# An adapter layer on one core: rows of 512 bytes for x and W, half of the first batch's x turned on VectorE, two reorderings at the third chunk and at the end

## What is computed

```
x = x + (x @ B0[id].T) @ A0[id].T                    # id: one of 64 adapters per batch, rank 16
logits = x @ Wr.T + 5 * one_hot(language)             # 8 experts
gates  = softmax over the two largest logits
x = x + x @ W.T + 2 * sum_e gates[e] * (x @ A[e].T) @ Bm[e].T    # rank 16, W is 2048 x 2048
```

## Time and profile before

| | us |
|---|---|
| median of 3 runs | 1563.22 (1560.31 to 1563.93) |
| the profiled execution | 1561.31 |
| its span | 1559.5 |

### The profile page before, as it was taken

The page is one execution under the profiler, slowest core; times in us unless marked ns, Lnnn a source line. Parts: engine busy times, 40 slices in busy tenths (PEclk is TensorE's granted clock), DMA queues, the critical chain, the costliest instruction groups (busy, mean ns, idle before and its releaser), DMA issues.

```text
span 1559.5 us, 20275 instructions
## 1 busy us (share of the span) xinstructions
PE 1541.5 (99%) x7430; PEld 1298.3 (83%) x7430; DVE 1230.4 (79%) x1692; ACT 714.2 (46%) x911; POOL 79.7 (5%) x119
## 2 busy tenths in 40 slices
PE   9989999999999999999999999999999999999998
PEld 8778878888888888888888888888888888888887
DVE  6998878977799767887688776997769976787665
ACT  6522222544445444455445444454444554445442
POOL 2333331000000000000000000000000000000000
PEclk9999999999999999999999999999999999999999
DMA  9899999787777767687676977667776777666564
GB/s 263 224 276 281 265 254 246 215 230 205 218 231 220 216 196 231 219 229 220 203 224 196 257 207 218 216 205 231 209 218 226 215 217 195 214 219 217 198 219 160
DMA packets 303109, 347.04 MB, mean 223 GB/s; under 512 B 204890, under 2 KB 236682, under 8 KB 302346
## 3 DMA queue, kind: packets, MB, share of 16 engines
q1 hardware_dynamic: 293602, 314.28, 69.8%
q0 software_dynamic: 9136, 30.94, 6.0%
q10 hardware_dynamic: 272, 0.52, 0.1%
HBM read 278.52 MB, written 66.72 MB: 221 GB/s over the span
## 4 chain that ended last, share of the span: by engine, by line
PE 88%; DVE 5%; SPq 4%; DMA 2%; issue 1%; ACT 0%; DVEq 0%; ACTq 0%
PE pb L804 26%; PE pb L805 26%; PE pb L806 26%; PE pb L378 4%; PE pb L380 3%; PE pb L533 2%; SPq L669 2%; SPq L292 2%; DVE raw L684 1%; DVE xl L558 1%; DMA out_dram<-ost 1%; DVE pool_a L540 1%; DMA raw<-in_L_cond_W_dram 0%; DMA an<-in_L_cond_A_dram 0%; PE pb L319 0%
## 5 line engine op out<-in xcount | busy, mean ns | idle before, releaser
L796 ACT CAST wh<-raw 128x1024 fp32r<-128x1024 f32 (+1 forms) x453 | 475.4, 1049 | 705.3 <-PE pb L806 670.9
L800 DVE TENSOR_TENSOR wl<-raw,wh 128x1024 fp32r<-128x1024 f32 (+1 forms) x453 | 552.1, 1219 | 261.3 <-ACT wh L796 260.0
L804 PE MATMUL pb<-wh,sh 128*128 128x512 f32 x1568 | 612.8, 391 | 0.5 <-DVE ost L858 0.5
L805 PE MATMUL pb<-wl,sh 128*128 128x512 f32 x1568 | 611.6, 390 | 0.0
L806 PE MATMUL pb<-wh,sl 128*128 128x512 f32 x1568 | 611.2, 390 | 0.0
L806 PEld LDWEIGHTS pb<-wh,sl 128*128 128x128 f32 x1568 | 294.3, 188 | 62.8
L804 PEld LDWEIGHTS pb<-wh,sh 128*128 128x128 f32 x1568 | 294.5, 188 | 56.2 <-DVE wl L800 0.9
L805 PEld LDWEIGHTS pb<-wl,sh 128*128 128x128 f32 x1568 | 294.6, 188 | 55.1
L378 PE MATMUL pb<-awb,xah 128*128 128x304 f32 x512 | 139.0, 305 | 0.3 <-DVE xal L355 0.3
L380 PE MATMUL pb<-awb,xal 128*128 128x256 f32 x512 | 134.6, 280 | 0.0
L804 PE MATMUL pb<-wh,xh 128*128 128x512 f32 x256 | 101.5, 396 | 0.8 <-DVE xl L558 0.8
(11 more groups left out here) (153 smaller groups left out, 1258.6 us busy)
## 6 DMA issues: line engine op xcount, KB each, us to landing
raw<-t_scr SPq DMA_DIRECT2D x392, 512.0 KB, 4.1
xst<-in_x_dram SPq DMA_DIRECT2D x448, 64.0 KB, 3.8
out_dram<-ost SPq DMA_DIRECT2D x72, 256.0 KB, 3.5
raw<-in_L_cond_W_dram SPq DMA_DIRECT2D x124, 128.0 KB, 5.3
raw<-bt_scr SPq DMA_DIRECT2D x28, 512.0 KB, 3.6
out_dram<-u SPq DMA_DIRECT2D x56, 256.0 KB, 2.9
t_scr<-raw POOLq DMA_DIRECT2D x32, 256.0 KB, 4.4
t_scr<-tst POOLq DMA_DIRECT2D x16, 512.0 KB, 6.7
```

The lines of the kernel that those rows point to most:

```text
L796: e.copy(pair_split(wh, g), pair_source(g)).then_inc(c_wh, 1)
L800: e.tensor_tensor(out=pair_split(wl, g), in0=pair_source(g), in1=pair_split(wh, g).bitcast(f32), op=ALU.subtract).then_inc(c_wl, 1)
L804: e.matmul(o, h, wh[:, g % RING, k, :], start=start, stop=False)
L805: e.matmul(o, h, wl[:, g % RING, k, :], start=False, stop=False)
```

## The change

1. x (batches 1 to 7), half of batch 0's x, W and B0's columns are loaded in rows of 512 bytes (128 numbers), where rows of 64 numbers were used. A row then holds two pairs of feature tiles: the transposes take every fourth number of a row (`r` and `h` in the patterns) where they took every second. The tile order of A, Wr, B0 and A0 follows.
2. In batch 0, blocks 1, 3, 5 and 7 of x are loaded in the stream layout by four DMAs each and turned by VectorE (`x_turn_first`); TensorE and ScalarE turn and copy only blocks 0, 2, 4 and 6.
3. W comes in 32 units of 512 KB. Two units make two slots, so `w_turn` of an even tile needs both. Units have three places in turn: `raw` 0 and 1 and `xst` 1 (units 2 and 3 lie in `xst2`). Turns of odd tiles, and two `x_turn` at once in odd slots, stand at the head of their slot. x of batch 1 then has one place in `xst`.
4. In slot 28 the evacuation of the third chunk's last two tiles stands before `pair_lo` in VectorE's list.
5. The last slot's matmuls are ordered by token tile, and the last sum and its stores are done tile by tile.

```diff
-        x_b = x.rearrange("b (h v j) (c k a n) -> b h c k a j v n", h=2, j=32, c=4, k=2, a=4)
-
-        def x_block(m):
-            return xst[:, m % 2, :, :].rearrange("p t n -> p (t n)")
+        x_b = x.rearrange("b (h v j) (c a n) -> b h c a j v n", h=2, j=32, c=4, a=4)
+
+
+        def x_block(n, m):
+            return xst[:, m % 2 if n > 1 else 0, :, :].rearrange("p t n -> p (t n)")
+
+        def wait_x(e, n, m):
+            if n == 1:
+                e.wait_ge(d_x[0], 64 * (m + 1))
+            else:
+                e.wait_ge(d_x[m % 2], (0 if m % 2 else 512) + 64 * (4 * (n - 2) + m // 2 + 1))
...
-            e.transpose(two(n, q, kp).rearrange("p (g j) -> p g j", g=16),
-                        x_block(m).rearrange("p (g i h) -> p h g i", g=16, h=2)[:, u % 2, :, :]).then_inc(c_xc, 1)
+            e.transpose(two(n, q, kp).rearrange("p (r v j) -> p r v j", r=2, v=8),
+                        x_block(n, m).rearrange("p (v i r h) -> p h r v i", v=8, r=2, h=2)[:, u % 2, :, :, :])\
+             .then_inc(c_xc, 1)
...
-            if n == 1 and m < 2:
-                if 0 in parts:
+            if n and 0 in parts:
+                if n == 1 and m == 0:
                     e.wait_ge(c_bt, 4)
-            elif n and 0 in parts:
-                e.wait_ge(c_xc, 16 * (n - 1) + 2 * m - 2)
-            if n == 0:
+                elif n == 1:
+                    e.wait_ge(c_xc, 2 * m)
+                elif n == 2 and m == 0:
+                    e.wait_ge(c_xc, 16)
+                elif n == 2 and m == 1:
+                    e.wait_ge(c_wc, 64)
+                else:
+                    e.wait_ge(c_xc, 16 * (n - 1) + 2 * m - 2)
+            if n == 0 and m % 2 == 0:
                 e.dma_start(x_place(m), x_v[0, half, :, :, cols * CW:(cols + 1) * CW]).then_inc(d_x0[m], 16)
+            elif n == 0:
+                for a in range(4):
+                    e.dma_start(x_place(m)[32 * a:32 * a + 32, :, :].rearrange("p t n -> p (t n)")
+                                .rearrange("p (v n) -> p v n", v=8), x_b[0, half, cols, a]).then_inc(d_x0[m], 16)
             else:
                 for a in parts:
-                    for k in range(2):
-                        e.dma_start(x_block(m)[32 * a:32 * a + 32, k * CW:(k + 1) * CW]
-                                    .rearrange("p (v n) -> p v n", v=8), x_b[n, half, cols, k, a])\
-                         .then_inc(d_x[m % 2], 16)
+                    e.dma_start(x_block(n, m)[32 * a:32 * a + 32, :].rearrange("p (v n) -> p v n", v=8),
+                                x_b[n, half, cols, a]).then_inc(d_x[m % 2 if n > 1 else 0], 16)
...
+        def kept_in(u):
+            return u // 4 * 2 + u % 2 + 1
...
-            if u >= 2:
-                wait_kept(e, 0, u - 2)
+            if u >= 4:
+                wait_kept(e, 0, u - 4)
...
-                    block = x_place(m)[:, t, :].rearrange("p (k n h) -> p k h n", k=2, h=2)[:, k, u % 2, :]
+                    block = x_place(m)[:, t, :].rearrange("p (n k h) -> p k h n", k=2, h=2)[:, k, u % 2, :]
...
-        def x_keep_dve(e, u):
+        def x_turn_first(e, u):
             q, kp = x_unit(u)
-            e.wait_ge(c_tr, u + 1)
-            e.tensor_copy(two(0, q, kp), pb[:, x_bank(u), :]).then_inc(c_x0[1], 1)
+            m = u // 2
+            if u % 2 == 0:
+                e.wait_ge(d_x0[m], 64)
+            e.transpose(two(0, q, kp).rearrange("p (r v j) -> p r v j", r=2, v=8),
+                        x_place(m).rearrange("p t n -> p (t n)")
+                        .rearrange("p (v i r h) -> p h r v i", v=8, r=2, h=2)[:, u % 2, :, :, :]).then_inc(c_x0[1], 1)
...
+        def unit_place(n):
+            if n in (2, 3):
+                return xst2[:, n - 2, :, :].rearrange("p t n -> p (t n)")
+            at = n if n < 2 else (n - 1) % 3
+            return (raw[:, at, :, :] if at < 2 else xst[:, 1, :, :]).rearrange("p t n -> p (t n)")
+
+        def unit_landed(e, n):
+            if n in (2, 3):
+                e.wait_ge(d_w2, 128)
+            elif n < 2:
+                e.wait_ge(d_w[n], 64)
+            else:
+                at = (n - 1) % 3
+                e.wait_ge(d_w[at], 64 * ((n - 1) // 3 + (at < 2)))
+
+
+        raw_w = W.rearrange("(c w g j) (q a n) -> c w q a j g n", c=4, w=2, j=32, q=4, a=4)
...
+        def unit_load(e, n):
+            if n in (2, 3):
+                wait_kept(e, 0, 13)
+                wait_kept(e, 0, 15)
+            elif n == 6:
+                e.wait_ge(c_bt, 4)
+            elif n in (4, 5):
+                e.wait_ge(c_wc, 4)
+            elif n > 6:
+                e.wait_ge(c_wc, 4 * ((n - 3) // 2) + 4)
+            landed = d_w2 if n in (2, 3) else d_w[n] if n < 2 else d_w[(n - 1) % 3]
+            for a in range(4):
+                e.dma_start(unit_place(n)[32 * a:32 * a + 32, :].rearrange("p (g n) -> p g n", g=8),
+                            raw_w[n // 8, n % 2, n // 2 % 4, a]).then_inc(landed, 16)
...
-            raw_landed(e, g)
+            for n in range(w // 2 * 2, w // 2 * 2 + 2):
+                unit_landed(e, n)
             if w >= 2:
                 e.wait_ge(c_wl, g - 2 - (g % 9 < 2) + 1)
                 wait_sums(e, w - 2)
                 e.wait_ge(d_bs[w % 2], 32 * (w // 2))
-            for h in range(2):
-                e.transpose(w_kept(g)[:, h, :].rearrange("p (g j) -> p g j", g=16),
-                            w_raw(g).rearrange("p (g i h) -> p h g i", g=16, h=2)[:, h, :, :])\
+            for n in range(2):
+                e.transpose(w_kept(g)[:, :, n * HT:(n + 1) * HT].rearrange("p h (g j) -> p h g j", g=8),
+                            unit_place(w // 2 * 2 + n).rearrange("p (g i r h) -> p r h g i", g=8, r=2, h=2)[:, k % 2, :, :, :])\
                  .then_inc(c_id if diagonal else c_wc, 1)
             if diagonal:
+                e.wait_ge(c_id, 4 * c + 2 * (k % 2) + 2)
                 for h in range(2):
-                    e.wait_ge(c_id, 4 * c + 2 * (k % 2) + h + 1)
-                    block = w_kept(g)[:, h, k % 2 * HT:(k % 2 + 1) * HT].rearrange("p (n h) -> p h n", h=2)[:, h, :]
+                    block = w_kept(g)[:, h, :].rearrange("p (n s) -> p s n", s=4)[:, k % 2 * 2 + h, :]
                     e.tensor_tensor(out=block, in0=block, in1=ident[:, :], op=ALU.add).then_inc(c_wc, 1)
...
+            if g == LAST - 1:
+                for t in range(2):
+                    toks = slice(t * P, (t + 1) * P)
+                    for k in range(2):
+                        last = three_products(e, pb[:, 2 * c + t, :], sh[:, h % SR, k, toks], sl[:, h % SR, k, toks], g, k,
+                                              False, k == 1)
+                    last.then_inc(c_sum, 1)
+                return
...
+            if is_last(b, product, c):
+                e.wait_ge(c_evd, evd_of(b, 5, c))
+                for t in range(2):
+                    e.wait_ge(c_sum, sum_of(b, product, c) + t)
+                    e.tensor_tensor(out=u2[:, c, t, :], in0=u2[:, c, t, :], in1=acc(c)[:, t, :], op=ALU.add)\
+                     .then_inc(c_evd, 1)
+                return
...
-                e.wait_ge(c_evd, evd_of(b, 6, c))
                 for t in range(2):
+                    e.wait_ge(c_evd, evd_of(b, 6, c) + (t if is_last(b, product, c) else 0))
...
-            e.transpose(columns_place(n)[:, CW:2 * CW].rearrange("p (h k j) -> p h k j", h=2, k=HK),
-                        columns_place(n)[:, 0:CW].rearrange("p (k i h) -> p h k i", k=HK, h=2)).then_inc(c_bt0, 1)
+            for h in range(2):
+                e.transpose(columns_place(n)[:, CW:2 * CW].rearrange("p (h c r j) -> p h c r j", h=2, c=4, r=2)[:, h, :, :, :],
+                            columns_place(n)[:, 0:CW].rearrange("p (c i r h) -> p h c r i", c=4, r=2, h=2)[:, h, :, :, :])\
+                 .then_inc(c_bt0, 1)
...
-            for u in range(2, 4):
-                x_transpose(e, u)
             for s in range(16):
-                if s < 12:
+                if s < 12 and (4 + s) // 2 % 2 == 0:
                     x_transpose(e, 4 + s)
...
+            for u in (2, 3):
+                x_turn_first(e, u)
             x_lo(e, 0, 2)
             for s in range(15):
-                if s < 12 and s % 2:
-                    x_keep_dve(e, 4 + s)
+                if s < 12 and (4 + s) // 2 % 2:
+                    x_turn_first(e, 4 + s)
...
-            for g in range(3):
-                first_load(e, g)
-            e.wait_ge(c_tr, 8)
+            for n in range(2):
+                unit_load(e, n)
+            wait_kept(e, 0, 5)
+            wait_kept(e, 0, 7)
             e.dma_start(bn, Bm.rearrange("e (p j) r -> p e j r", p=P)).then_inc(d_bn, 16)
-            first_load(e, 3)
+            for n in range(2, 4):
+                unit_load(e, n)
             e.wait_ge(c_ar, 2)
             e.wait_ge(c_pool, 5)
             for row, part in G_ROWS:
```

(40 more changed lines are left out.)

90 lines of the change are left out of this document (33 added, 57 removed).

## The result

The changed kernel takes 1605.72 us (median of 4 runs, 1604.90 to 1606.88), the kernel before beside it 1561.76 (4 runs): ratio 1.0282, 95% interval 1.0264 to 1.0299. It is 44 us slower; the forecast was 16.5 us slower, 1578. The profiled execution took 1604.9 us, its span is 1603.1.

The account below looks back on a forecast made before the run. TensorE, busy 1541.5 of 1559.5 us, bounds the kernel, with VectorE also full until 101 us. Terms 1.6+7.0+4.6+4.3+0-1.0 = +16.5 us on the profiled 1561.3 gave 1578 us; range 1557 to 1590.

Parts of the forecast that it names:

- The step: Every VectorE transpose reading at 16 bytes in place of 8 takes d = 0.50 us longer, range 0 to 0.60.
- Head: To 47.3 us: 2.5 us of 5.2 us TensorE lead real, against turn 0.6, transposes 3.0, adds 0.5: sum +1.6 us.
- Slots 0 to 6: To the gate, with VectorE full: seven tiles of two slower transposes, 14 x d = +7.0 us.
- Slots 7 to 9: Up to xal 0: tiles 11 and 12, columns_turn and the turns of x 0 and 1 add +4.6 us.
- Slots 10 to 24: VectorE work 2.8 us more than its idle time fits, plus 1.5 us (0 to 4) for late W: +4.3 us.
- Third chunk: Delta's 2.6 us stall on L858 goes, but turns in slots 28 to 33 give it back: 0, -2.6 to +3.
- Batches 2 to 7: Later batches: longer rows of x give nothing, TensorE is full and VectorE has 38 us of room per batch.
- Tail: End of the kernel: half of the last sum and the first store issue lie beside the last products, -1.0 us.
- What would show it: Signs: transposes 1.1 to 1.3 us, hg wait about 11, xal waits about 7, L858 wait gone, sum halves 0.69.
- The faster one: Rival: the 16-byte step costs nothing on VectorE, -4.7 us, 1557 to 1558 us; chance 0.24.
- much slower: Rival: d over 0.6 and later batches run late, 1 to 3 us each, 1592 us and more; chance 0.04.
- The clock as an upper end: TensorE at 1.2 GHz behind the 4.4 us stall: a longer stall can lengthen that; in the upper end, not the sum.

Follow-up runs that it names:

- the fills: The changed kernel with filling transposes of ident on TensorE before hg of batch 0 and before five aux products of batch 1: 1608.94 us, ratio 1.0300.

## Why the prediction was wrong, step by step

The direction was right, and so was the step of the transposes as a term: it is some 20 of the 44 us. The size was not, because the prediction left out a wait of another kind, for x on SP's queue. Measured steps are from the profiled executions. (The forecast names 1.9 us between the profiled execution and the median and does not add them; with them it would have been 1579.7 us.)

- **The step.** The extra time d of a transpose was taken as 0.50 us and measured as 0.39 (1072 against 682 ns), within 0 and 0.60. The forecast's way of summing it was right to the gate and too low in all: 10 us in the kernel before, 18 to 20 in the changed one.
- **Head, +1.6, measured +7.0.** Failed, in the term of the lead. From the start of w_turn 0 to the end of the second a0_rows_lo I had +4.1 us, and it is +3.6 (35.40 to 47.56 us against 31.68 to 40.24). "So I take 2.5 us of the 5.2 as real" put w_turn 0 that much earlier. It starts 3.7 us later: the last loads of x leave SP's queue at 23.6 us where they had left it at 15.8, W is issued 7.7 us later behind them, and VectorE waits 2.2 us for it. Batch 0's x as before gives 5.0 us back.
- **Slots 0 to 6, +7.0, measured +6.4** (13.4 less 7.0). Near, in part by luck: 14 times 0.39 is 5.5, and with the step taken back 2.1 us remain in this stretch, for which the forecast had no term.
- **Slots 7 to 9, +4.6, measured +3.2** (16.6 less 13.4). Right within the range of d.
- **Slots 10 to 24, +4.3, measured +22.1** (38.7 less 16.6). This is the step that failed. I compared VectorE's work with its idle time and put 1.5 us (0 to 4) on late units of W. I did not follow x on SP's queue: one place, its load behind eight issues that wait for `w_turn`. That makes turn, W's issues, x's issue and landing one row of steps per two slots, with the queue's wait in it. 11.5 us come back by moving x's issue, 13.5 by not loading it. Without those loads the same stretch grows by 6.2 us (25.0 less 18.8), near the 4.3 of the sum: what it counted was about right, and the wait for x is what it left out.
- **Third chunk, 0 (up to +3), measured +3.9** (first product of batch 1 at 316.99 against 274.37 is +42.6, less 38.7). The 2.6 us stall of delta on L858 is gone, and in its place TensorE waits 4.6 us for `adapt`. The same trade, 1.2 and 1.3 us for 2.6, is what the reordering does alone in the kernel before. With the reordering in and the step, the head and the loads of x taken back, the wait for `adapt` is 2.2 us. So the turns hold it up too, as the upper bound had it.
- **Batches 2 to 7, 0.** VectorE is busy 154.12 us of 186 in a batch (318 to 504 us), TensorE 185.97: no cost is seen there. The last gate is 2.3 us later than the first product of batch 1 gives; the runs of before spread over 4 us, so whether this is the change's stays open.
- **Tail, -1.0, measured -1.3**: from the start of the last matmul to the end are 3.8 us against 5.1. Its sums in the changed kernel, to be held against the earlier trace rows:

```profile
1598.43 0.69 DVE L962 TENSOR_TENSOR u<-u,pb 128x512 f32<-128x512 f32 x1 [4.54 <-PE pb L830]
1599.69 0.69 DVE L962 TENSOR_TENSOR u<-u,pb 128x512 f32<-128x512 f32 x1 [0.57 <-PE pb L830]
```

- **What would show it.** The turns at 1.1 us came. The wait before hg, put at 11 us, is 5.2 only: TensorE came late itself, by the head and by its waits on the way. The waits for xal, put at 7 us, are 16.3.
- **Rivals.** The faster one fell with the 1072 ns. The "much slower" one named the wrong place: the later batches had room, the slots 10 to 24 had not. The clock as an upper end was right as a sign (12.6 against 3.0 us), but the fills show no separate price between the aux products of batch 1, and elsewhere it stays open.

## What to carry to other kernels

Fewer, longer rows on DRAM's side are paid for on the reading engine's side: on VectorE up to 8 bytes from one f32 number to the next are free (711 ns for 512), and 16 cost half as much again (1078). Before engines' busy times are compared with their room, follow each buffer whose places are cut through the queue that refills it: place free, what stands ahead on that queue and waits for what, issue, landing. And a stall of the busiest engine may be the slack of a transfer: the 4.4 us before hg could be shortened to 1.5 and nothing came of it. Take a stall away alone before building on it.
